# Gated cross-attention with a top-2 expert layer: attention scores as fp32 matmuls on 32-row strips in place of a stack of bf16 parts

## The reference

```python
v = values.reshape(N, v_len, HEADS, HEAD_DIM)      # values = keys = ctx_1024
energy = jnp.einsum('nqhd,nkhd->nhqk', q, k)       # q = layernorm(x)
attn = jax.nn.softmax(energy / jnp.sqrt(jnp.float32(EMBED_SIZE)), axis=3)
out = jnp.einsum('nhql,nlhd->nqhd', attn, v).reshape(N, q_len, EMBED_SIZE)
return out @ w_out.T + b_out
...
x = x + jnp.tanh(g_xattn[0]) * _L0_xattn_ref(ctx_1024, ctx_1024, _layernorm(x, axis=-1), w_out, b_out)
x = x + jnp.tanh(g_ffn[0]) * _L0_ffn_ref(_layernorm(x, axis=-1), Wg, W1, b1, W2, b2)
```

## Time and profile before

| what | before |
|---|---|
| time, median of 3 runs | 539.84 us (537.06 to 541.55) |
| span of the profiled execution | 518.6 us |
| median minus that span | 21.2 us |
| PE, DVE, ACT, POOL busy in the span | 69%, 64%, 47%, 43% |
| attention stage, by the windows | 0 to about 310 us |
| expert stage | about 330 to 485 us |
| rest | final gather, sum and stores |

### The profile page before, as it was taken

One profiled execution on the slowest core, in us unless ns is written; L12 is line 12 of the kernel. 1 busy time (PEld: TensorE's weight loads), 2 busy tenths in 40 slices (PEclk: granted clock), 3 DMA queues, 4 the chain that ended last, 5 costly groups with the idle time before them and its releaser, 6 DMA issues. The chain is left out here.

```text
span 518.6 us, 14516 instructions
## 1 busy us (share of the span) xinstructions
PE 359.4 (69%) x3754; PEld 306.3 (59%) x3755; DVE 331.5 (64%) x1264; ACT 244.8 (47%) x708; POOL 224.4 (43%) x353
## 2 busy tenths in 40 slices
PE   1227685768877766968676850599999999999500
PEld 0115464557656554746555630589999999899500
DVE  3745576787788778688776766254545555455377
ACT  2316474656566465657554420255555555455300
POOL 4431214554545355454545463044545554455400
PEclk9997787896798779698878775599999999999855
DMA  7786655535454453344344212222222222222096
GB/s 207 187 133 101 111 90 103 110 66 100 83 91 82 81 107 80 68 97 91 58 72 93 73 33 63 52 57 57 61 60 59 63 64 59 54 58 61 11 294 186
DMA packets 73594, 46.38 MB, mean 89 GB/s; under 512 B 7606, under 2 KB 68440, under 8 KB 73568
## 3 DMA queue, kind: packets, MB, share of 16 engines
q1 hardware_dynamic: 68640, 37.37, 33.8%
q0 software_dynamic: 4352, 8.43, 6.2%
q10 hardware_dynamic: 576, 0.26, 0.2%
HBM read 18.02 MB, written 15.83 MB: 65 GB/s over the span
## 5 line engine op out<-in xcount | busy, mean ns | idle before, releaser
L796 DVE TENSOR_REDUCE negmax<-bank 128x4 bf16<-128x512 f32 x128 | 88.5, 702 | 57.4 <-PE bank L632 56.8
L589 ACT ACTIVATE hT<-bank,ex_cur 128x128 f32<-128x128 f32 x288 | 82.3, 369 | 78.9 <-PE bank L733 72.2
L523 POOL DMA_INDIRECT choice_rows<-y_s,dest x72 | 78.5, 1090 | 94.0 <-DVE y_s L950 85.0
L566 ACT ACTIVATE probs<-bank 128x512 f32<-128x512 f32 x128 | 73.3, 598 | 91.7 <-PE bank L619 90.7
L619 PE MATMUL bank<-stack 128*128 128x128 bf16 x512 | 55.6, 256 | 53.2 <-DMA stack<-mT 40.4
L733 PE MATMUL bank<-xtT,ex_cur 128*128 128x128 f32 x576 | 82.0, 286 | 3.5 <-DVE xtT L945 2.0
L747 PE MATMUL bank<-w_sb,hT 128*128 x576 | 81.1, 284 | 0.4 <-ACT hT L589 0.4
L733 PEld LDWEIGHTS bank<-xtT,ex_cur 128*128 128x128 f32 x576 | 71.4, 195 | 9.8 <-DVE xtT L945 8.1
L619 PEld LDWEIGHTS bank<-stack 128*128 128x128 bf16 x512 | 36.5, 113 | 68.5 <-DMA stack<-mT 39.1
L506 POOL DMA_INDIRECT expert_rows<-xrow,slot_i x64 | 64.8, 1013 | 18.6 <-issue 18.6
L747 PEld LDWEIGHTS bank<-w_sb,hT 128*128 128x128 f32 x576 | 70.6, 193 | 1.9 <-issue 0.8
(11 more groups left out here) (127 smaller groups left out, 542.9 us busy)
## 6 DMA issues: line engine op xcount, KB each, us to landing
stack<-parts SPq DMA_DIRECT2D x192, 64.0 KB
xt<-expert_rows SPq DMA_DIRECT2D x72, 64.5 KB, 1.8
choice_rows<-zeros SPq DMA_DIRECT2D x16, 256.0 KB, 4.1
stack<-choice_rows SPq DMA_DIRECT2D x16, 256.0 KB, 5.3
ex_sb<-in_L_ffn_W_dram SPq DMA_DIRECT2D x4, 512.0 KB, 5.9
w_sb<-in_L_ffn_W_dram SPq DMA_DIRECT2D x4, 512.0 KB, 5.2
out_dram<-x_all SPq DMA_DIRECT2D x8, 256.0 KB, 3.8
x_all<-in_x_dram SPq DMA_DIRECT2D x5, 384.0 KB, 5.2
```

Of the source, the lines that this page charges most:

```text
L523: nc.gpsimd.indirect_dma_start(y_dram, bass.IndirectOffsetOnAxis(ap=dest[:, v, :], axis=0), y_s[:, v, :], None, bounds_check=last_row, oob ...
L566: nc.scalar.activation(probs[:, b.slot, g, :], E_BANK[g % 2][:, :], ACT.Exp, scale=SCALE).then_inc(exp_done, 1)
L589: last = nc.scalar.activation(hT[:, v % 2, c, :], H_BANK[v % 2][:, c * P:c * P + P], ACT.Gelu, bias=ex_cur[:, v, FF + D + c:FF + D + c + 1])
L796: V.tensor_reduce(negmax[:, m.slot, J * g:J * g + J], S_BANK[g % 2][:, :].rearrange("p (j k) -> p j k", j=J), AX.X, ALU.max, negate=True). ...
```

## The change

The parts, the stack and all seven DMAs per sequence go. The transposed keys are kept as they are in fp32 (`kT`); the transposed queries are kept four times (`qT`, index `j`), each time multiplied on ACT by `head_mask`, a column that is 1 on the eight rows of one head in every group of 32 rows and 0 elsewhere. A strip of 32 partitions thus holds four heads, and the product of a strip of `kT` with a strip of the `j`-th masked copy is the score of one head. The main scores are one fp32 matmul per strip, 32 rows by 512 columns, followed by four bf16 matmuls per strip that add the maxima (`pick` selects one row of `mT`). The maxima come from bf16 matmuls on the upper halves of the same fp32 numbers (`kT_high`, `qT_high`). Strips are taken in pairs that write to two different PSUM banks. DVE takes the maximum of two banks in one instruction of 1024 columns. The work of a pair is ordered anew on each engine, `m` and all later letters come one step earlier, and the whole pipeline is unrolled.

```diff
-    MAX_ROW = 96
+    KQ = 3
...
-        parts = sb("parts", [P, 2, 2 * len(TERMS), P], BF16)
-        rest = sb("rest", [P, 2, 2, P])
-        stack = sb("stack", [P, 4, H, 2 * P], BF16)
+        kT = sb("kT", [P, KQ, P])
+        qT = sb("qT", [P, KQ, J, P])
...
-            BEHIND = (1, 0, -2, -3, -4, -5, -6, -7, -8)
+            BEHIND = (1, 0, -1, -2, -3, -4, -5, -6, -7)
+            for t in range(-1, B - min(BEHIND)):
+                step(*[t + k if 0 <= t + k < B else None for k in BEHIND])
...
@@ SP, step @@
-                if b:
-                    sp.wait_ge(mT_ready, at(b, 1, 1))
-                    sp.dma_start(stack[MAX_ROW:MAX_ROW + 1, b.place, :, 0:P], mT[:, b.slot, :]).then_inc(mT_in[b.slot], 16)
-                if a:
...
-                    for t in range(len(TERMS)):
-                        sp.dma_start(stack[HD * t:HD * t + HD, a.place, :, :],
-                                     parts[:, a.slot, 2 * t:2 * t + 2, :].rearrange("p b q -> p (b q)")).then_inc(stack_in[a.slot], 16)
+                if a is not None and a >= 2:
+                    sp.wait_ge(qkT_ready, a)
+                    side_transfer(a - 2)
@@ ACT, step, between exp(1) and exp(2) @@
+                if a is not None:
+                    act.wait_ge(qkT_psum, at(a, 1, 1))
+                    wait(act, e_ready, at(a, G, -2 * G))
+                    nc.scalar.copy(kT[:, a % KQ, :], TA[:, P:2 * P])
+                    for j in range(J):
+                        last = nc.scalar.activation(qT[:, a % KQ, j, :], TA[:, 0:P], ACT.Copy, scale=head_mask[:, j:j + 1])
+                    last.then_inc(qkT_ready, 1)
@@ PE, step @@
+                def max_scores(h):
...
+                    pe.wait_ge(qkT_ready, at(m, 1, 1))
+                    wait(pe, max_done, at(m, 2, h))
+                    for j in range(J):
+                        for g in (2 * h, 2 * h + 1):
+                            strip = slice(32 * g, 32 * g + 32)
+                            last = nc.tensor.matmul(S_BANK[g % 2][:, j * P:j * P + P], qT_high[strip, m % KQ, j, :],
+                                                    kT_high[strip, m % KQ, :], start=True, stop=True)
+                    last.then_inc(s_ready, 1)
+                def main_scores(h):
...
+                    pe.wait_ge(mT_ready, at(b, 1, 1))
+                    wait(pe, exp_done, at(b, G, 2 * h))
+                    for g in (2 * h, 2 * h + 1):
+                        strip = slice(32 * g, 32 * g + 32)
+                        nc.tensor.matmul(E_BANK[g % 2], kT[strip, b % KQ, :], qT[strip, b % KQ, :, :].rearrange("p j q -> p (j q)"),
+                                         start=True, stop=False, skip_group_check=True)
+                    for j in range(J):
+                        for g in (2 * h, 2 * h + 1):
+                            strip = slice(32 * g, 32 * g + 32)
+                            last = nc.tensor.matmul(E_BANK[g % 2][:, j * P:j * P + P], pick[strip, j, :], mT[strip, b % 2, :],
+                                                    start=False, stop=(j == J - 1), skip_group_check=True)
+                            if j == J - 1:
+                                last.then_inc(e_ready, 1)
@@ DVE, step @@
-                        V.tensor_reduce(negmax[:, m.slot, J * g:J * g + J], S_BANK[g % 2][:, :].rearrange("p (j k) -> p j k", j=J),
-                                        AX.X, ALU.max, negate=True).then_inc(max_done, 1)
+                    V.tensor_reduce(negmax[:, m % 2, 2 * h:2 * h + 2, 0:J], S_ALL[:, :].rearrange("p (g j k) -> p g j k", g=2, j=J),
+                                    AX.X, ALU.max, negate=True).then_inc(max_done, 1)
...
-                    V.memset(stack[:, n.place, :, 0:P], 0.0).then_inc(stack_free, 1)
```

More of the change, by code:

```diff
@@ L17 @@
-from collections import namedtuple
 from contextlib import ExitStack
@@ L34 @@
 GATE_EPS = 1e-9
[L38 to L56, removed]
 def flamingo_layer(nc, x, ctx, g_xattn, g_ffn, w_out, b_out, Wg, W1, b1, W2, b2, out):
@@ L279, in cols, with chunk_due, pipeline @@
         def cols(s, width=P):
[L281 to L295, removed]
-            BEHIND = (1, 0, -2, -3, -4, -5, -6, -7, -8)
[L301 to L311, removed]
+            return slice(s * width, s * width + width)
+        def chunk_due(s):
+            return CHUNKS.index(s) if s in CHUNKS[:-1] else None
+        def pipeline(step):
+            BEHIND = (1, 0, -1, -2, -3, -4, -5, -6, -7)
+            for t in range(-1, B - min(BEHIND)):
+                step(*[t + k if 0 <= t + k < B else None for k in BEHIND])
         def write_pads(eng, experts):
@@ L506, in step @@
                         nc.gpsimd.indirect_dma_start(
-                            xs_dram, bass.IndirectOffsetOnAxis(ap=slot_i[:, d.place, k:k + 1], axis=0),
-                            xrow[:, d.place, k, :], None).then_inc(row_out[d.place], 16)
-                if n and first_quad(n):
-                    nc.gpsimd.memset(stack[:, n.place, :, P:2 * P], 1.0).then_inc(stack_ones, 1)
-            pipeline(pool, step)
+                            xs_dram, bass.IndirectOffsetOnAxis(ap=slot_i[:, d % 4, k:k + 1], axis=0),
+                            xrow[:, d % 4, k, :], None).then_inc(row_out[d % 4], 16)
+            pipeline(step)
             pool.wait_ge(zeroed, 16 * NZ)
@@ L707, in step @@
                     for k in range(2):
[L708 to L709 removed]
+                        nc.tensor.matmul(R_BANK[:, 64 + k * E:64 + k * E + E], before[:, k, :], chosen[:, r % 2, k, :], start=True, stop=True)
+                        last = nc.tensor.matmul(R_BANK[:, 96 + k * E:96 + k * E + E], every[:, k, :], chosen[:, r % 2, k, :], start=True, stop=True)
                     last.then_inc(cum_ready, 1)
[L711 to L714 removed]
+                if m is not None:
+                    pe.wait_ge(max_done, at(m, 2, 2))
+                    if r is not None:
+                        pe.wait_ge(xn2T_ready, at(r, 1, 1))
+                    nc.tensor.transpose(TB_max, negmax[:, m % 2, :, :].rearrange("p g j -> p (g j)"), ident_b[:, :]).then_inc(m_psum, 1)
+            pipeline(step)
             pe.wait_ge(table_done, 1)
```

365 lines of the change are left out of this document (146 added, 219 removed).

## The result

| | before | after |
|---|---|---|
| median of 4 runs each, us | 538.45 (534.44 to 541.55) | 599.59 (588.47 to 603.87) |
| ratio, 95% interval | | 1.102 (1.091 to 1.114) |
| span of the profiled execution, us | 518.6 | 586.6 |
| mean granted clock, whole span | not recorded | 0.705 |

The forecast was 508 us, between 488 and 545, with 0.15 for slower. It was wrong. The ratio of an experiment is made with runs of the kernel before on the same chip. Which chip the result above was measured on is not recorded. The experiments fell on five chips, here A to E; on D that kernel takes 517.7 us, on the others 535 to 537. Some executions of a kernel are over 1.5% longer than its fastest, at a lower clock; the ratios leave them out (so 1.102 and not 599.59 / 538.45 = 1.114), the medians keep them, and the profiles of `e2`, `e9`, `e15` and `e17` are of such executions.

A forecast was written before the change was run, and what follows sets the result against it. It took the attention stage to be bound by DVE's work, or by DMAs where these come late. Span 518.6 - 19 (steps) - 13 (start) = 487; time 539.8 - 32 = 508 us, range 488 to 545.

The forecast's parts named there:

- rival 3: Attention stage: PE's clock stays at 0.80, averaged step 8.6 us, total 532 us; chance 0.13.
- a cold step of 10.3: Attention step at half clock: PE's parts double, adding 1.9 us to the path, about 10.3 us.
- Strips side by side: Main scores: a pair of fp32 strip matmuls runs at once, two rounds in 0.87 us, against 1.75 one after another.
- The full-clock step: Attention pipeline: one step at full clock takes 7.75 us against 8.46, saving 19 us over 27 steps.
- DVE's maximum of 1024 columns: DVE in the attention step: one maximum over 1024 columns lasts 1.24 us, 1.15 to the next start.
- its wait for it: DVE idle about 1.6 us before each first maximum, released by PE's first scores.
- What follows the last `xrow`: Expert stage (300 to 480 us) and the end: stay as they are.
- The start: First pipeline steps: memset, maxima's DMA and one step less, against half-clock fp32; net 13 us saved, between 6 and 18.
- Five ACT copies: ACT, keys and four masked queries: 0.9 us if scaling costs nothing, at twice that 1.8, still inside DVE's time.
- the drain: End of the attention pipeline, the last four `xrow` starts: left at 19.7 us.
- Unrolling: Whole pipeline: fewer register instructions, longer program; counted as nothing, up to 0.2 us a step either way kept for the range.
- Rival 4: Attention step: faster `xn` and shorter chain around the quotient save 0.6 us, step 7.15, total 492 us; chance 0.12.

The follow-up runs named there:

- e2: Changed kernel with the fp32 main scores over all 128 rows instead of a 32-row strip (changes the computation): 600.4 us, ratio 1.119.
- e9: `e1` with the first half's maxima moved to the head of PE's step, ahead of the attn transpose: 504.3 us, ratio 0.931.
- e15: `e8` with one filler matmul a step in place of three, on chip D: 467.8 us, ratio 0.903.
- e17: `e15` run again on chip E: 511.9 us once and 542.7 to 549.4 three times, kernel before 536.2.
- e3: Changed kernel with both main-score matmuls of a pair, and their bf16 matmuls, on the same 32-row strip (changes the computation): 714.1 us, ratio 1.332.
- e1: Changed kernel plus three unread full-row filler matmuls (bf16, 512 columns) a step: 508.9 us, ratio 0.951.
- e16: The kernel before, unchanged, run and profiled on chip E: 535.7 us, ratio 1.000.
- e7: The kernel before with its attention pipeline fully unrolled and nothing else changed: 529.7 us, ratio 0.986.
- e8: `e1` with the first half's maxima issued on PE ahead of its main scores: 496.6 us, ratio 0.918.
- e10: Changed kernel without filler, with the first half's maxima at the head of PE's step: 530.1 us, ratio 0.975.

## Why the prediction was wrong, point by point

**The step that failed** is the argument against rival 3: "what PE waited for before its drops was DMA, and the new step has no PE wait above a microsecond and more PE work". It took the clock to follow PE's busy share. The share did rise, from 39.57 to 42.75 of 50 us, and the clock fell from 0.80 to 0.65 and 0.50. The change moves the longest matmuls of a step onto 32 of 128 rows, two at a time, and a step made of such matmuls did not hold 2.4 GHz (`e2` against `e3`; three full-row matmuls a step bring it back, `e1`).

**The price of that rival** (532 us, a cold step of 10.3) was too low twice over. The clock did not stay at 0.80 but went to 0.59, and a cold step lasts 11.97. The 10.3 counted DVE's chain with PE's parts of it doubled. In the window from 200 to 300 us PE is busy 88.04 us for 8.4 steps, 10.5 us each: at 1.2 GHz PE's own row is the bound, with ACT's late copy behind it. At full clock PE has time to spare in a step (`e1` does three matmuls more in 7.72 us); at half clock all of its work counts. The reason why rows count is not shown, only that they do.

**What held.** Strips side by side: two rounds of fp32, `pick` starting 0.96 us after the first record (forecast 0.87); four records last 1.13 us to the end of the last, in series 1.88 (`e2`). The full-clock step 7.81 (7.75). DVE's maximum of 1024 columns 1.22 us (1.24), its wait for it 1.85 (1.6). What follows the last `xrow` unchanged. The start gained 9 of 13 us, within its 6 to 18.

**What was right by luck.** The forecast added 21.2 us to the span, the distance between the median and a profile. In the result that distance is 588.47 - 586.6 = 1.9 us, and in every run of the kernel before since it is 2 to 3; so the profile of before is of an execution of about 521 us, near the 517.7 of chip D, and was held against times of a slower chip. With the clock restored, `e1` took 508.9 us against the forecast 508, but the profiled span is 503.5 us against a forecast 487. Against the profile of `e16` (chip E, whose kernel before is within 0.1% of chip A's) its start is 9.0 us earlier and its steps take 17.2 us less from first to last `xrow`: 26.1 us saved of the 32 forecast.

**What was off by size.** Five ACT copies take 1.32 us (77.95 to 79.27) in place of 0.9, inside the bounds and hidden. The last four starts of `xrow` lie 25.8 us apart in all, not the 19.7 at which the drain was left. Unrolling, counted as nothing, was a gain of 5 us by the medians (`e7`), about the 0.2 us a step kept for it. Rival 4, a shorter chain around the quotient, has a counterpart in `e8`.

**What was not on the list.** Late writes: not in the trace of before, so no row could have priced them. They widen the loss in time but hardly the ratio (1.102 with them, 1.098 without, in the looped form).

**What stays open.** Rows are not all that counts: `e15` and `e17`, one kernel, had clocks of 1.00 and 0.67 on two chips, and `e10` 0.69 without filler. How the clock depends on the amount of full-row work was measured at a few points only: three matmuls a step were enough on A and C (fewer weren't tried there), one on D, and one wasn't on E. What one gives on D is not separated from the order of `e8`, which no run had without filler. Whether late writes are what makes one too few on E, and whether they make up all of the 3.5% between D and the others, wasn't separated: no run took all of them away on those chips.

## What to carry to other kernels

Before moving matmuls onto row strips, ask what then keeps TensorE's clock: the busy share does not show it, the granted clock does, and a step priced at full clock needs its price at half clock beside it, with each engine's whole row of work. If the clock falls, try a few full-row matmuls in PE's idle places; here three a step turned +10% into -5%, and with the maxima moved ahead into -8%. And profile the kernel before on the chip that times it: chips differed by 3.5% here, and one profile had waits that another hadn't.

## What the runs showed of the hardware

- PE busy 94% with its main matmuls on one 32-row strip at a time had a granted clock of 0.53 (`e3`); busy 75% with the fp32 ones on all rows, 0.88 (`e2`).
- Work that nobody reads shortened a kernel by 15% (599.6 to 508.9 us; the kernel before took 538.5 and 535.8 us beside them, so 14% by the ratios).
- On four of five chips many of PE's semaphore writes came 0.2 to 2.8 us late while GpSimd issued an indirect DMA or just after, and on the fifth the attention had none; the kernel before took 535 to 537 us on the four and 517.7 us on the fifth.
